# Selective-state recurrence, attention and experts on one core: the recurrence's front two iterations earlier, Silu in two sessions, result rows found on GpSimd, 110 tiles instead of 112

## The reference

```python
# 1. selective state space (E = 512 channels, N = 16 states)
x = rmsnorm(resid) * norm_w
skip = x @ skip_w.T;  x = x @ in_w.T
x = silu(causal_conv4(x) + conv_b)
delta = softplus(x @ Wd1.T @ Wd2_w.T + Wd2_b)
Bm, Cm = x @ WB.T, x @ WC.T
h = exp(delta * A) * h + (delta * x) * Bm     # a step for each token
y = sum_n(h * Cm) + x * W_D
y = (y * silu(skip)) @ out_w.T
x = layernorm(resid + (resid + y))
# 2. cross-attention, 16 heads of 16, rotary positions, residual, layernorm
# 3. 15 experts, each token goes to its best 3, and a shared expert:
#    fc2(gelu(gate half) * other half), weighted sum, residual, layernorm
```

## Time and profile before

| | us |
|---|---|
| median of 3 runs (lowest to highest) | 2185.69 (2179.36 to 2189.15) |
| the profiled execution | 2181.16 |
| its span, first to last instruction | 2179.3 |

### The profile page before, as it was taken

The page is one execution under the profiler, slowest core; times in us unless marked ns, Lnnn a source line. Parts: engine busy times, 40 slices in busy tenths (PEclk is TensorE's granted clock), DMA queues, the critical chain, the costliest instruction groups (busy, mean ns, idle before and its releaser), DMA issues. The chain is left out here.

```text
span 2179.3 us, 32460 instructions
## 1 busy us (share of the span) xinstructions
PE 1697.8 (78%) x9684; PEld 1089.3 (50%) x9685; DVE 1588.5 (73%) x2792; ACT 1042.0 (48%) x2354; POOL 1248.0 (57%) x840
## 2 busy tenths in 40 slices
PE   5688778778777778534787888777498999999695
PEld 4344444444444444213455555555385555555484
DVE  3699999999899999965478888875223555555278
ACT  3677777777777777620233333333112333333221
POOL 0889888898889899847547776633200222222100
PEclk9899998999899999657799999988699999999897
DMA  5544444555554455414833333331541222222332
GB/s 162 116 115 114 113 111 108 116 117 117 117 117 116 103 123 114 111 60 97 211 106 109 123 105 113 110 106 38 177 163 36 79 82 82 80 81 82 139 128 77
DMA packets 178820, 238.24 MB, mean 109 GB/s; under 512 B 24001, under 2 KB 114113, under 8 KB 176642
## 3 DMA queue, kind: packets, MB, share of 16 engines
q1 hardware_dynamic: 161426, 201.73, 35.4%
q0 software_dynamic: 9984, 28.06, 3.6%
q10 hardware_dynamic: 7280, 6.83, 1.2%
HBM read 169.70 MB, written 66.84 MB: 109 GB/s over the span
## 5 line engine op out<-in xcount | busy, mean ns | idle before, releaser
L268 POOL TENSOR_TENSOR inject<-dx_n,bc_n 128x2048 f32<-128x2048 f32 x128 | 578.9, 4533 | 147.5 <-DMA dx_n<-dup_rows 84.7
L401 ACT ACTIVATE ps_h<-delta_n,a_neg 128x256 f32<-128x256 f32 x1024 | 424.9, 462 | 110.9 <-DVE hc L537 73.5
L524 DVE TENSOR_TENSOR_SCAN ps_h<-ps_h,inject 128x1024 f32<-128x1024 f32 x160 | 365.9, 2287 | 23.8 <-ACT ps_h L401 23.8
L1951 POOL DMA_INDIRECT token_results<-e_y,e_y_row x112 | 106.9, 955 | 389.8 <-DVE e_y L2013 389.5
L1114 ACT ACTIVATE expT<-ps_t 128x512 f32<-128x512 f32 x256 | 147.6, 593 | 307.9 <-PE ps_t L1496 305.7
L1192 DVE TENSOR_REDUCE neg_max<-ps_s 128x2 f32<-128x512 f32 x256 | 172.2, 676 | 123.4 <-PE ps_s L1485 122.9
L524 DVE TENSOR_TENSOR_SCAN h_pool<-ps_h,inject 128x1024 f32<-128x1024 f32 x96 | 218.6, 2278 | 18.9 <-POOL inject L268 14.5
L277 POOL TENSOR_TENSOR h_pool<-h_pool,bc_n 128x1024 f32<-128x1024 f32 x96 | 225.7, 2351 | 0.0
L2041 PE MATMUL e_ps_h<-w,e_xT 128*128 x448 | 219.5, 613 | 7.7 <-issue 6.6
L537 DVE TENSOR_TENSOR hc<-ps_h,bc_n 128x1024 f32<-128x1024 f32 x160 | 195.7, 1223 | 5.9
L1485 PE MATMUL ps_s<-Ks,Qs 96*128 96x256 bf16 x512 | 103.8, 286 | 45.4 <-DVE neg_max L1192 34.9
(11 more groups left out here) (274 smaller groups left out, 3453.0 us busy)
## 6 DMA issues: line engine op xcount, KB each, us to landing
delta_n<-dup_rows SPq DMA_DIRECT2D x128, 256.0 KB, 4.6
dx_n<-dup_rows SPq DMA_DIRECT2D x128, 256.0 KB, 7.6
bc_n<-bc_rows SPq DMA_DIRECT2D x64, 256.0 KB, 4.5
xg<-slot_rows SPq DMA_DIRECT2D x112, 136.0 KB, 2.1
Ks<-k_rows SPq DMA_DIRECT2D x192, 64.0 KB
Qs<-q_rows SPq DMA_DIRECT2D x192, 64.0 KB
e_rows_in<-token_results SPq DMA_DIRECT2D x8, 1536.0 KB, 18.9
dup_rows<-delta SPq DMA_DIRECT2D x32, 256.0 KB, 6.4
```

The lines of the kernel that those rows point to most:

```text
L268: nc.gpsimd.tensor_tensor(inject[:, at:at + 2, :, :], dx_n[c // 2][:, None, :, c % 2, :].to_broadcast([P, 2, JB, L]), bc_n[b % 2][:, 0, nq ...
L401: last = nc.scalar.activation(ps_h[k % 2][:, j, :], delta_n[c // 2][:, j, c % 2, :], ACT.Exp, scale=a_neg[:, c, nq, j:j + 1])
L524: nc.vector.tensor_tensor_scan(out.rearrange("p j t -> p (j t)"), ps_h[k % 2][:, :, :].rearrange("p j t -> p (j t)"), inject[:, k % RING, ...
L1951: g.indirect_dma_start(out=y_dram, out_offset=bass.IndirectOffsetOnAxis(ap=y_row[:, j:j + 1], axis=0), in_=y[j][:, 0, :], in_offset=None). ...
```

## The change

- The front of b+1 and the entry of b+2 stand two iterations earlier on all engines. All four convolutions of a sequence are done in the sequence before (i = 13, 14, 15, 15).
- `silus` (i = 0) makes only u; `silu_skip` (i = 1) makes silu(skip). Each loads both tables, four loads a sequence. `skip` has three buffers. `silus` waits for the sums that last read the buffer of u, not for the gate.
- `take_delta` of the first half comes ahead of `softplus_log` of the second. `normalize` moves from i = 13 to 14.
- The residual is added in place in X (no `res`), and `xn` lies in half of `zln`, so `norm_x` also waits for the softplus sum that reads it; `norm_x(1)` in the prologue moves behind the deltas.
- `expert_phase`: 110 tiles, the last six (t = 104 to 109) unrolled behind the same 25 looped rounds. The row numbers come ready in the slot rows (the filler rows hold dump rows, made on the host), and GpSimd converts them, `find_rows(t+2)` ahead of `send(t)`, with a semaphore that the load of a later x tile also waits for. VectorE loses the code copy and the maximum, and does `take_y(t)` before `multiply(t+2)`.
- Filler and spare rows come from DRAM constants and not from a zeroed tile; `lane` has one column.

```diff
-SLOT_TILES = (T * TOPK // P + NE + 1) // 2 * 2
+SLOT_TILES = T * TOPK // P + NE - 1
+SKIPS = 3
+SPARE_TILES = SLOT_TILES - T * TOPK // P
+DUMP_TILES = NE + SPARE_TILES
...
-        xn = sb("xn", [P, TT, D])
-        skip = [sb(f"skip{j}", [P, EC, L]) for j in range(2)]
+        skip = [sb(f"skip{j}", [P, EC, L]) for j in range(SKIPS)]
+        xn = zln[:, 0:2, :]
-        res = sb("res", [P, TT, D])
...
             def norm_x(b):
                 if b >= 1:
                     act.wait_ge(f_tr, b)
+                    act.wait_ge(f_sp, (b - 2) * 2 + 3 if b >= 2 else 1)
                 for s in range(TT):
                     t = b * TT + s
                     last = nc.scalar.activation(xn[:, s, :], X[:, t, 0:D], ACT.Copy, scale=rstd[:, t:t + 1])
...
                 act.preload_act_table_set("silu_and_others")
                 act.wait_ge(f_skip_raw, b * 2 + 2)
                 if b >= 2:
-                    act.wait_ge(gated, (b - 1) * EC)
+                    act.wait_ge(s_sum, hc_count((b - 2) * ITERS + ITERS - 3))
                 for n, c in enumerate(CONV_ORDER):
                     if n % 2 == 0:
                         act.wait_ge(f_conv, b * 2 + n // 2 + 1)
                     nc.scalar.activation(u[q][:, c, :], (ps_b if c // 2 else ps_a)[:, c % 2, :], ACT.Silu,
                                          bias=conv_b[:, c:c + 1]).then_inc(f_u, 1)
-                nc.scalar.activation(skip[q][:, :, :], skip_raw[:, :, :], ACT.Silu).then_inc(f_u, 1)
+                act.preload_act_table_set(EXP_LN)
+
+            def silu_skip(b):
+                act.preload_act_table_set("silu_and_others")
+                if b >= SKIPS:
+                    act.wait_ge(gated, (b - SKIPS + 1) * EC)
+                nc.scalar.activation(skip[b % SKIPS][:, :, :], skip_raw[:, :, :], ACT.Silu).then_inc(f_u, 1)
                 act.preload_act_table_set(EXP_LN)
 
...
                 act.wait_ge(row_step, row(b, SHIFT))
                 for s in range(TT):
-                    last = nc.scalar.activation(X[:, b * TT + s, 0:D], res[:, s, :], ACT.Identity,
+                    last = nc.scalar.activation(X[:, b * TT + s, 0:D], X[:, b * TT + s, 0:D], ACT.Identity,
                                                 scale=r2[:, s:s + 1], bias=shift[:, s:s + 1])
                 last.then_inc(x_made, 1)
...
             silus(0)
-            norm_x(1)
+            silu_skip(0)
             take_db(0)
             for hf in range(2):
                 softplus_exp(0, hf)
                 softplus_log(0, hf)
             take_delta(0, 0)
             take_delta(0, 1)
+            norm_x(1)
             root(REST, 1)
             scale_xT(1)
...
                 make_decay(k + 2)
+                if front and i == 0:
+                    silus(b + 1)
+                if front and i == 1:
+                    silu_skip(b + 1)
                 if front and i == 2:
-                    silus(b + 1)
+                    take_db(b + 1)
+                if front and i in (3, 5):
+                    softplus_exp(b + 1, (i - 3) // 2)
                 if front and i == 4:
-                    take_db(b + 1)
-                if front and i in (5, 7):
-                    softplus_exp(b + 1, (i - 5) // 2)
-                if front and i in (6, 8):
-                    softplus_log(b + 1, (i - 6) // 2)
+                    softplus_log(b + 1, 0)
+                if front and i == 6:
+                    take_delta(b + 1, 0)
+                    softplus_log(b + 1, 1)
                 if tail and i == 7:
                     layernorm_root(b - 1)
-                if front and i in (8, 10):
-                    take_delta(b + 1, (i - 8) // 2)
+                if front and i == 8:
+                    take_delta(b + 1, 1)
+                if entry and i == 7:
+                    norm_x(b + 2)
                 if entry and i == 9:
-                    norm_x(b + 2)
-                if entry and i == 11:
                     scale_xT(b + 2)
+                if entry and i in (10, 11):
+                    take_xin(b + 2, i - 10)
                 if entry and i in (12, 13):
-                    take_xin(b + 2, i - 12)
-                if entry and i in (14, 15):
-                    take_skip(b + 2, i - 14)
-                if tail and i == 13:
+                    take_skip(b + 2, i - 12)
+                if tail and i == 14:
                     normalize(b - 1)
             layernorm_root(B - 1)
...
-                nc.vector.tensor_tensor(y_gated[:, c, :], ps_y[c % 2][:, 0, :], skip[b % 2][:, c, :],
+                nc.vector.tensor_tensor(y_gated[:, c, :], ps_y[c % 2][:, 0, :], skip[b % SKIPS][:, c, :],
                 v.wait_ge(out_done, b + 1)
-                if b >= 1:
-                    v.wait_ge(x_made, b)
-                nc.vector.scalar_tensor_tensor(res[:, :, :], X[:, b * TT:(b + 1) * TT, 0:D], 2.0, ps_y[1][:, :, :],
-                                               ALU.mult, ALU.add).then_inc(row_step, 1)
+                at = X[:, b * TT:(b + 1) * TT, 0:D]
+                nc.vector.scalar_tensor_tensor(at, at, 2.0, ps_y[1][:, :, :], ALU.mult, ALU.add).then_inc(row_step, 1)
...
                 if b > 0 and 5 <= i < 14 and rows[i - 5] is not None:
                     rows[i - 5](b - 1)
-                if b < B - 1 and i in (9, 11):
-                    make_dx(b + 1, (i - 9) // 2)
+                if b < B - 1 and i in (7, 9):
+                    make_dx(b + 1, (i - 7) // 2)
             gate(B - 1, EC - 1)
             for step in rows:
...
-            conv(1, 0)
+            for n in range(EC):
+                conv(1, n)
             for k in range(B * ITERS):
                 b, i = divmod(k, ITERS)
                 front, entry, tail = b < B - 1, b < B - 2, b > 0
                 sums(b, i)
-                if front and i in (0, 1):
-                    conv(b + 1, i + 1)
-                if front and i == 1:
-                    conv(b + 1, 3)
+                if front and i == 2:
+                    project_db(b + 1)
                 if tail and i == 3:
                     project_out(b - 1)
-                if front and i == 4:
-                    project_db(b + 1)
-                if front and i == 5:
+                if front and i == 3:
                     half_z(b + 1, 0)
                     half_z(b + 1, 1)
-                if front and i in (7, 9):
-                    add_softplus(b + 1, (i - 7) // 2)
-                if entry and i == 10:
+                if front and i in (5, 7):
+                    add_softplus(b + 1, (i - 5) // 2)
+                if entry and i == 8:
                     transposes(b + 2)
+                if entry and i in (9, 10):
+                    project_in(b + 2, i - 9)
                 if entry and i in (11, 12):
-                    project_in(b + 2, i - 11)
-                if entry and i in (13, 14):
-                    project_skip(b + 2, i - 13)
+                    project_skip(b + 2, i - 11)
+                if entry and i >= 13:
+                    conv(b + 2, i - 13)
                 if entry and i == 15:
-                    conv(b + 2, 0)
+                    conv(b + 2, 3)
             sums(B, 0)
             project_out(B - 1)
...
-                    sp.wait_ge(zero_made, 1)
-                    sp.dma_start(zero_v[:, NE * REGION:NE * REGION + spare, :],
-                                 ffn.zero[:, :].unsqueeze(1).to_broadcast([P, spare, XW])).then_inc(zeroed, 16)
+                    sp.dma_start(slots_dram[NE * REGION * P:, :], dram["spare_rows"]).then_inc(zeroed, 16)
...
-                sp.dma_start(slots_dram[bass.ds(at, P), :], ffn.zero[:, :]).then_inc(tail_filled, 16)
+                sp.dma_start(slots_dram[bass.ds(at, P), :], ffn.fill[:, :]).then_inc(tail_filled, 16)
...
-        code, y_row = sb("e_code", [P, R]), sb("e_y_row", [P, R], mybir.dt.uint32)
+        ROWS = 2 * R
+        y_row = sb("e_y_row", [P, ROWS], mybir.dt.uint32)
...
                 if t >= R:
                     sp.wait_ge(e_hid, t - R + 1)
+                    sp.wait_ge(e_rows, t - R + 1)
                 load_x(t, t)
 
             def step(i, j, left):
                 t = i * R + j
                 if left > R + AHEAD:
                     sp.wait_ge(e_hid, t + AHEAD + 1)
+                    sp.wait_ge(e_rows, t + AHEAD + 1)
                     load_x(t + R + AHEAD, j + AHEAD)
 
             steps(sp, step)
...
         def _(g):
-            for t in range(SLOT_TILES):
+            def find_rows(t):
+                at = t % ROWS
+                e = expert(g, t)
+                g.wait_ge(x_in[t % R], 16 * (t // R + 1))
+                if t >= ROWS:
+                    g.wait_ge(y_out[t % R], 16 * ((t - ROWS) // R + 1))
+                nc.gpsimd.tensor_copy(y_row[:, at:at + 1], xg[t % R][:, bass.ds(e + D, 1)]).then_inc(e_rows, 1)
+
+            def send(t):
                 j = t % R
+                g.wait_ge(e_rows, t + 1)
                 g.wait_ge(e_y, t + 3)
```

(40 more changed lines are left out.)

19 lines of the change are left out of this document (8 added, 11 removed).

## The result

The changed kernel took 2187.68 us (median of 20 runs, 2182.07 to 2191.16) against 2179.46 (2175.81 to 2189.87, 20 runs) of the kernel before: ratio 1.0031, 95% interval 1.002 to 1.0042. It is slower by 0.3%, inside what I had called no change, while I had forecast 13 us less. (The forecast of 2173 us started from the median of three runs, 2185.69, which lies 6 us above the median of twenty.) The stage that I had wrong is the recurrence.

A forecast was written before the change was run, and what follows sets the result against it. It took VectorE's work and waits to bound the recurrence, and VectorE's serial chain the expert loop. Recurrence +11, prologue +1.7 and experts -25.8 gave -13 us, from the median 2185.69 to 2173 us; range 2160 to 2194.

The forecast's parts named there:

- The stalls of Silu: Recurrence: the two half sessions on ScalarE stall VectorE 1.64 us before scan 3 and 1.86 before scan 4, each sequence.
- The rest of the front moves by two iterations with unchanged order between engines: Recurrence front: the 1.16 us wait before dx goes; the second `make_dx` finds delta an estimated 0.15 us late.
- the prediction's sum for a sequence: Recurrence, VectorE's waits: 1.64 + 1.86 + 0.15 = 3.65 us a sequence against 3.0 before.
- The prologue: Before the first dx: two more table loads, 2.56 us, less norm_x of sequence 1, 0.91: +1.7 us.
- The experts: Expert stage: a round of 12.6 us, two tiles fewer, GpSimd's copy hidden at 0.7 us; -25.8 us in all.
- The reason behind the expert sum: Expert loop: VectorE's serial lap of 3.24 us falls to 2.5, below TensorE's 3.02, so TensorE becomes the bound.
- 3: Rival, recurrence: ScalarE's stalls cascade to db and half z, TensorE's clock falls; 30 us more, +17, 2203 us; chance 0.16.
- my +11: Recurrence: waits of 54.8 us against 45.4 over 15 sequences, plus 1.5 in the first; ends +3 and +30.
- 1: Rival, expert loop: it stays where it is and only 6.6 us go; +6 in all, 2192 us; chance 0.16.
- 2: Rival, recurrence: both Silu halves and dx hide, so 45.4 us go; -69 in all, 2116 us; chance 0.07.
- 4: Rival, expert loop: GpSimd's copy and register load take over 1.8 us and set it; +46, 2245 us; chance 0.06.
- 5: Rival, ScalarE: it stands still 1.28 us beside each table load; +77, 2250 us; chance 0.02.

The follow-up runs named there:

- rec_only: The kernel before with only the changed recurrence phase (`mamba_phase`), expert stage left at 112 tiles: 2217.76 us, ratio 1.0167 to the kernel before.
- one_session: The changed kernel with Silu in one session at iteration 0, two table loads a sequence: 2163.86 us, ratio 0.9911 to the kernel before.

## Why the prediction was wrong, point by point

- **The stalls of Silu: right.** 1.64 and 1.86 us predicted, 1.59 and 1.79 found, 30 times; before dx 0.2 us in all instead of 0.15 a sequence. In all I expected 54.8 us, and 1.5 in the first sequence; 51.3 came.
- **"The rest of the front moves by two iterations with unchanged order between engines": this step failed.** The front and the entry moved, but the iterations that GpSimd weighs (`POOL_HC`) and the two buffers of `h_pool` did not. Two iterations earlier, TensorE's wait for xnT stands ahead of the sum of iteration 8, whose buffer scan 12 needs, and the idle stretch puts `project_in` at the lower clock level; the prediction's sum for a sequence has no term for either. That is 23.3 us, and it is nearly the whole error: waits of 51.3 + 23.3 = 74.6 against the old 45.4 is +29, the row of the table says +28.8. I had counted what stands behind a moved wait on ScalarE (norm_x, decay 10, take_delta), and not on TensorE.
- **The prologue: +3.3, not +1.7.** Both loads are on that path, as assumed: TensorE waited 3.38 us for db, against 1.47 before. Most of the rest is its clock: it ran the two products of the half z in 2.07 and 1.91 us, against 1.13 and 1.03 (rows in the last section). In rec_only, with the same code and the same 3.38 us of waiting, they took 1.13 and 1.03, and the first scan came at 66.7 and not at 69.4. With one session it came at 64.4.
- **The experts: right in size.** A round of 12.67 against 12.6; the stage -22.3 against -25.8. Of the missing 3.5 us, 1.8 are the 0.07 a round, the rest lies in the tiles outside the loop. That GpSimd's conversion is hidden was right; the instruction alone takes 0.20 us, and the 0.7 that I took had the register load in it.
- **The reason behind the expert sum: half right.** Taking the copies off VectorE moved the bound. The lap of 3.24 us that I read has no wait for TensorE, but once a round, in before too, VectorE waits some 0.8 us for the up product (19.2 us in 24 rounds); four such laps would make 12.96 us, and the round took 13.33. That `take_y` first helps was argued, and in the kernels with short rounds it did not: 4 to 5 us slower on the front of before, under 1 us in the changed kernel.
- **Rivals.** 3 came nearest: the recurrence lost 18 us more than my +11, where it had 30 more. Of its mechanism the clock was right: the granted clock of the recurrence fell from 0.89 to 0.86, and the slow `project_in` is part of the wait; over the whole kernel it was 0.894, and 0.902 once that wait was gone. The place was not: the extra wait is for the entry of b+2, not for db or the half z of the front, and it sits in front of one scan. 1 had nearly the total, +6 against the measured +8, but by luck: the expert loop did get shorter, and a loss elsewhere made up for it. 2 and 4 did not occur. 5 did not either: with four loads a sequence instead of two, each took 1.28 us and 0.01 us followed it, so the drain that the Trainium skill states (ScalarE: Activation LUTs, What ACT_TABLE_LOAD costs) does not show in this trace either.

## What to carry to other kernels

When a block of work is moved by n iterations, list everything that stays where it is (which iterations use which buffer, which queue holds which wait) and lay it beside the moved waits: on each engine, ask who waits for what stands behind them. A small reorder on the engine that is late can be worth more than shifting everything earlier: three lines on ScalarE gave 20 us, where the whole earlier front cost 28 as first written and gave 4 to 5 once both its faults were mended. And a change of several parts that moves the time little should be cut into its stages first; here two runs showed -30 and +35. Read their stage rows too: 5.6 and 7.5 us of these lay in stages where no line was changed.

## What I had not expected of the hardware

- TensorE's clock can make a wait cost more than itself: after 4.00 us idle, at a granted clock of 0.50, `project_in` took 3.78 us for eight products, where the second half took 1.99 at 1.00 soon afterwards. A wait of 4 us became a delay of 4.00 + 3.78 - 1.99 = 5.8. The length of the idle time alone does not decide it: 3.47 us was followed by 1.99 in one_session, 2.84 us by 1.99 in rec_only and by 3.44 in the changed kernel. The prologue shows the same; before:

```profile
37.50 1.13 PE L675 MATMUL ps_a<-db,w_d 97*128 97x256 f32 x4 [1.47 <-ACT db L347]
38.47 1.03 PE L675 MATMUL ps_b<-db,w_d 97*128 97x256 f32 x4
```

  and after:

```profile
40.01 2.07 PE L688 MATMUL ps_a<-db,w_d 97*128 97x256 f32 x4 [3.38 <-ACT db L356]
41.87 1.91 PE L688 MATMUL ps_b<-db,w_d 97*128 97x256 f32 x4
```

  The granted clock is 1.00 from 37.5 to 39.5 before and 0.50 from 40.0 to 43.8 after. In rec_only it stayed at 1.00 behind the same wait, so most of the 2.7 us between the first scans of rec_only and the changed kernel (66.7 and 69.4) is the clock, not the wait.

- The same instructions in one stage took 12.55 or 12.66 us a round, and 13.33 or 13.57, in programs that differ elsewhere. The same recurrence took 884.7 or 879.1 us from first to last scan, and there VectorE's waits name the difference: 60.3 us of idle time against 54.6. Differences of 3 to 8 us between single profiles of this kernel need a timed run, or a wait that names them.
